# Late block tables, low parts and the shared tile of a routed decoder layer, placed anew

## The chip, the cores and the metric

The kernel runs on one core of one Trainium2 chip. The time is device microseconds of that core for the whole program, from the inputs in HBM to the output in HBM. Below, PE is TensorE, DVE is VectorE, ACT is ScalarE, POOL is GpSimd and SP is SyncE; all times inside the profiled execution are us from the start of its span.

## What is computed

One post-norm decoder layer on 1024 tokens of width 256, in fp32:

```
x = layernorm(x + attention(x))
x = layernorm(x + expert_of_token_id(x))      # 4 experts made from ctx_2048
g = silu(x @ Wg[e]);  u = x @ Wu[e];  y = (g * u) @ Wd[e]
# e: the expert with the highest router probability, 1 of 4, d_ff = 1024
x = layernorm(x + y * probability[e])
```

The change touches only the last block, the routed feed-forward with its four experts.

## The kernel before

**Tiles and items.** The tokens have been sorted by expert into a table in HBM (`x2_sorted`), in blocks of 128 rows of one expert. The last block works on T2 = 10 tiles, 0 to 9. Tiles 0 to 8 hold a block each; the last one, tile 9 (`JOINT`), is shared by two half blocks of 64 rows, which may be of two experts. The hidden width of 1024 is cut into NQ = 4 quarters. The work list `items` has 40 entries: for each quarter, tiles 0 to 9. An item is: up projection (`fup`), silu on ACT (`fsilu`), product with the second half on DVE (`fhidden`), turn of the hidden tile on PE (`fth`), its split into a high and a low part (`fhhi` on ACT, `fhlo` on DVE), down projection (`fdown`), and the sum of the quarters on DVE (`fsum`; in the last quarter `finish`, which also takes the moments of the last layernorm).

**Split precision.** Matrix products of tiles 0 to 8 are three products each: high x high, high x low, low x high (the lines 563 to 565 in `split_mm`). The weights come as 16 chunks (4 experts x 4 quarters, 768 KB each) into three staging buffers (`stage`). A chunk is split in 3 pieces of 512 columns: ACT writes the high part to `w_hi` (line 930), POOL subtracts and writes the low part to `w_lo` (line 474). A quarter has 12 pieces. The list `share` says how many of the next quarter's pieces go behind each item of this quarter. Chunks 0 to 6 are in SBUF before the block begins; chunk 7 holds the last three pieces (the 10th to 12th) of the second quarter. The first item of a quarter waits until all low parts of that quarter are there.

**The shared tile** is multiplied in plain fp32 with weights of its own (`w32`, two transfers of 768 KB per quarter from `load_w32`), as 8 up and 8 down products on 64 columns of the array (`fup_joint`, lines 825; `fdown_joint`, line 836).

**Order written out by hand.** Every engine runs a loop over i. In step i, PE does `ftx(i+1)` (turns the next tile's rows; first quarter only), `fup(i)`, `fth(i-1)`, `fdown(i-2)`; ACT does `fxhi(i+1)`, `fsilu(i)`, `fhhi(i-1)`, then the pieces of `share`; DVE does `fxlo(i+1)`, `fhidden(i)`, `fhlo(i-1)`, then `fsum(i-2)` or `finish(i-2)`. Step 3 (`EARLY`) has an order of its own, since the rows of tile 3 come late. In steps 34 to 43 ACT also writes the normed rows (`norm_row`, line 1059) of the item four steps back, and POOL sends each finished tile to HBM with an indirect DMA (line 552), with a power of -1/2 for a later tile between them (`root`, line 478).

**Tables.** Which block a tile takes is computed on DVE. Tiles 3 to 5 (`late_tables`, then `late_offsets`) just before step 0; tiles 6 to 10 in `last_rows` at the end of step 1 (its five instructions: two for `block_table`, two for `wrapped`, one for `row_table_of`, lines 1306 to 1317); the two experts of the shared tile in `joint_tables` in step 3. The semaphore `row_table` tells SP how many of these are there: 2 is tiles 3 to 5, 3 is tiles 6 to 10, 4 is the shared tile's experts.

**SP's queue.** SP issues, strictly in this order: rows of tiles 3 to 5 behind `row_table` 2; rows of tiles 6 and 7 behind `row_table` 3; behind `row_table` 4 the two `w32` transfers, the rows of tile 8, the two halves of the rows of tile 9; then chunk 7 and the later chunks (line 329). Each row transfer (132 KB) needs its row number loaded from SBUF into a register first.

## Time and profile before

| | |
|---|---|
| median of 3 runs | 188.86 us (188.37 to 189.16) |
| the profiled execution: its own time | 189.77 us |
| its span, first to last instruction | 186.9 us |
| PE busy | 169.5 us, 91% of the span |
| PE weight loads busy | 127.6 us, 68% |
| DVE / ACT / POOL busy | 126.5 / 98.0 / 101.3 us |
| the last block, steps 0 to 41 on PE | 72.4 to 178.1 us |
| granted TensorE clock, mean | 0.982 (full until 180, half behind it) |

The profiled execution is 0.91 us longer than the median. About 2.8 us of its time lie outside the span. Busy shares are averages over stages with different limits; what a change in one stage is worth is read from the waits of that stage. PE's busy share counts a matmul's latency, and neighbouring matmuls overlap in it, so steps are measured from start to start.

### The profile page before, as it was taken

What the parts mean: (1) busy time and instruction counts of PE and PEld (TensorE: products, weight loads), DVE (VectorE), ACT (ScalarE), POOL (GpSimd) and SP (SyncE); (2) the same over time, 40 slices, a digit from 0 to 9 for tenths busy, and PEclk for the clock granted to TensorE, in tenths of its full rate; (3) what the DMA queues carried; (4) which work ended last, traced back from release to release, by engine and by line L of the source; (5) the groups of instructions that cost most, each with busy time, mean ns of one, the idle gap of its engine ahead of it and who ended that gap; (6) DMA issues with size and microseconds to landing.
All of it is one profiled execution on the core that took longest, in us unless ns stands there. A gap on an engine that the chain in (4) does not pass through costs nothing.

```text
span 186.9 us, 3756 instructions
## 1 busy us (share of the span) xinstructions
PE 169.5 (91%) x944; PEld 127.6 (68%) x944; DVE 126.5 (68%) x411; ACT 98.0 (52%) x252; POOL 101.3 (54%) x127
## 2 busy tenths in 40 slices
PE   7999998899989979799899999999999999999800
PEld 2678766468868736478686788857888677887500
DVE  3489776868778958868544464443699965888740
ACT  3258889345476543357553966652666422344430
POOL 8100766626636646557745097860688810266683
PEclk9999999999999999999999999999999999999975
DMA  5999998347999341236982475455670003511020
GB/s 139 366 339 414 381 381 340 114 129 216 388 321 407 124 122 34 76 91 226 328 298 96 150 315 172 168 168 172 256 249 5 0 0 106 234 55 57 22 81 12
DMA packets 14580, 35.28 MB, mean 189 GB/s; under 512 B 1886, under 2 KB 8416, under 8 KB 14434
## 3 DMA queue, kind: packets, MB, share of 16 engines
q1 hardware_dynamic: 12880, 31.84, 49.1%
q0 software_dynamic: 1392, 3.22, 4.7%
q8 instruction: 9, 0.15, 0.3%
q14 instruction: 9, 0.07, 0.1%
q10 hardware_dynamic: 290, 0.01, 0.1%
HBM read 26.57 MB, written 9.15 MB: 191 GB/s over the span
## 4 chain that ended last, share of the span: by engine, by line
PE 62%; DVE 15%; issue 6%; DMA 6%; POOL 5%; ACT 1%; SPq 1%; POOLq 1%; DVEq 0%; ACTq 0%
PE bank L563 12%; PE bank L565 12%; PE bank L564 11%; PE bank L740 6%; DMA rows<-x_sorted 4%; PE bank L846 4%; PE bank L717 4%; PE bank L825 3%; PE bank L571 3%; POOL rstd L478 2%; DVE stats L1202 2%; DVE buf L1199 2%; POOL out_tokens L552 2%; PE bank L836 2%; DMA x_sorted<-buf,slot 2%
## 5 line engine op out<-in xcount | busy, mean ns | idle before, releaser
L474 POOL TENSOR_TENSOR w_lo<-stage,w_hi 128x512 fp32r<-128x512 f32 x40 | 51.5, 1309 | 32.9 <-ACT w_hi L930 28.0
L1046 ACT ACTIVATE gate<-bank 128x256 f32<-128x256 f32 x40 | 15.4, 385 | 47.3 <-PE bank L565 39.8
L1453 DVE TENSOR_TENSOR hid<-bank,gate 128x256 f32<-128x256 f32 x40 | 17.0, 424 | 29.9 <-ACT gate L1046 29.7
L563 PE MATMUL bank<-w_hi,xr 128*128 x72 | 30.0, 416 | 1.3 <-issue 0.8
L564 PE MATMUL bank<-w_lo,xr 128*128 x72 | 28.4, 394 | 0.0
L565 PE MATMUL bank<-w_hi,xr 128*128 x72 | 28.4, 394 | 0.0
L930 ACT ACTIVATE w_hi<-stage 128x512 fp32r<-128x512 f32 x45 | 26.7, 631 | 1.7 <-DMA stage<-in_w_ffn 1.1
L478 POOL TENSOR_TENSOR rstd<-mv,mhalf 128x1 f32<-128x1 f32 x18 | 10.9, 608 | 28.2 <-DVE mv L1192 27.2
L563 PE MATMUL bank<-w_hi,hT 128*128 x72 | 23.3, 323 | 0.0
L565 PE MATMUL bank<-w_hi,hT 128*128 x72 | 20.3, 281 | 0.0
L564 PE MATMUL bank<-w_lo,hT 128*128 x72 | 20.2, 281 | 0.0
L563 PEld LDWEIGHTS bank<-w_hi,xr 128*128 128x128 f32 x72 | 13.5, 188 | 5.6 <-issue 3.8
L846 PEld LDWEIGHTS bank<-ident,hid 128*128 128x128 f32 x80 | 10.6, 140 | 9.5 <-issue 4.6
L846 PE MATMUL bank<-ident,hid 128*128 128x128 f32 x80 | 15.6, 277 | 1.2 <-issue 0.9
L518 POOL DMA_INDIRECT x_sorted<-buf,slot x11 | 11.1, 1006 | 8.5 <-DVE slot L1301 3.9
L565 PEld LDWEIGHTS bank<-w_hi,xr 128*128 128x128 f32 x72 | 13.5, 188 | 3.1
L1461 DVE TENSOR_TENSOR hT<-bank,hT 128x256 fp32r<-128x256 f32 x36 | 15.0, 416 | 0.3 <-ACT hT L1054 0.3
L564 PEld LDWEIGHTS bank<-w_lo,xr 128*128 128x128 f32 x72 | 13.6, 189 | 1.6
L571 PE MATMUL bank<-ones 128*128 128x512 bf16 x47 | 13.2, 432 | 1.1 <-POOL ones L426 1.1
L563 PEld LDWEIGHTS bank<-w_hi,hT 128*128 128x128 f32 x72 | 13.6, 189 | 0.2 <-issue 0.2
L564 PEld LDWEIGHTS bank<-w_lo,hT 128*128 128x128 f32 x72 | 13.7, 190 | 0.0
L552 POOL DMA_INDIRECT out_tokens<-buf,outidx x10 | 10.3, 1031 | 6.2 <-issue 3.8
(214 smaller groups left out, 349.7 us busy)
## 6 DMA issues: line engine op xcount, KB each, us to landing
stage<-in_w_ffn SPq DMA_DIRECT2D x15, 768.0 KB
arena<-in_w_ffn SPq DMA_DIRECT2D x8, 768.0 KB, 4.9
rows<-x_sorted SPq DMA_DIRECT2D x20, 132.0 KB, 2.7
x_sorted<-xr SPq DMA_DIRECT2D x2, 1056.0 KB, 6.8
x_sorted<-xr SPq DMA_DIRECT2D x1, 1584.0 KB
buf<-in_x_tok SPq DMA_DIRECT2D x1, 1024.0 KB, 10.5
w_hi<-in_ctx SPq DMA_DIRECT2D x1, 1024.0 KB, 11.5
w_hi<-in_ctxT SPq DMA_DIRECT2D x1, 1024.0 KB
```

Source lines behind the costliest of these rows:

```text
L474: g.tensor_tensor(out=lo, in0=src, in1=hi.bitcast(F32), op=ALU.subtract).then_inc(split_lo, 1)
L478: g.tensor_tensor(out=rstd[:, buf, i:i + 1], in0=mv[:, buf, i, 1:2], in1=mhalf[:, 0:1], op=ALU.pow).then_inc(rstd_ready, 1)
L552: g.indirect_dma_start(out=out, out_offset=bass.IndirectOffsetOnAxis(ap=outidx[:, t:t + 1], axis=0), in_=buf[:, t, 0:D], in_offset=None, b ...
L563: mm(dst, xhi, whi, start=start, stop=False)
L564: mm(dst, xhi, wlo, start=False, stop=False)
L565: return mm(dst, xlo, whi, start=False, stop=stop)
L571: mm(bank[2][:, :].rearrange("p (a b) -> p a b", a=4), ones[:], idle_rhs, start=True, stop=True)
L846: last = tr(fH[j % 2][:, k * P:(k + 1) * P], hid[:, (T + j) % 2, k * P:(k + 1) * P], ident[:])
L930: a(hi, src, ACT.Copy).then_inc(split_hi, 1)
L1046: a(gate[:, (T + j) % 2, :], fA[j % 2][:, 0:FQ], ACT.Silu).then_inc(silu_done, 1)
L1453: v.tensor_tensor(out=hid[:, (T + j) % 2, :], in0=fA[j % 2][:, FQ:2 * FQ], in1=gate[:, (T + j) % 2, :], op=ALU.mult).then_inc(h_done, 1)
L1461: v.tensor_tensor(out=hT[:, j % 2, 1, :], in0=fH[j % 2][:, 0:FQ], in1=hT[:, j % 2, 0, :].bitcast(F32), op=ALU.subtract).then_inc(hlo_done, 1)
```

## The change

Three things, and what goes with them:

1. **Tables.** `late_offsets` (tiles 3 to 5) moves from before step 0 into step 1, behind `fxlo(2)`. `last_rows` is cut in two: `last_blocks` (two instructions) stays in step 1, the other three stay under the name `last_rows` and move to step 3, behind `fxlo(4)` and ahead of `joint_tables`. On SP the rows of tile 8 move from behind the `w32` transfers to behind those of tile 7.
2. **Pieces.** `share` becomes a list for each quarter. In the first quarter pieces begin in step 2 and go as 1, 1, 2, 2, 2, 2, 2; in the second and third they begin with the quarter's first item and end with one piece in its ninth. ACT's wait before it overwrites a half of `w_hi` asks for one item less (`y_done` ... - 1), since the shared tile doesn't read `w_hi`.
3. **Last quarter.** The order of tiles becomes 0 to 5, 9, 6, 7, 8 (`last_order`). `finish`, `norm_row` and the stores count by place n and take the tile from `last_order`.

Nothing is added to the arithmetic: each engine has as many instructions as before.

```diff
--- before.py
+++ after.py
@@ -305,16 +305,21 @@
         Q_PIECES = E * PIECES
 
 
-        share = [0, 1, 2, 1, 2, 1, 2, 1, 2, 0]
-        assert sum(share) == Q_PIECES and len(share) == T2
-
-        def quarter_pieces(q, t):
-            a = q * Q_PIECES + sum(share[:t])
-            return range(a, a + share[t])
+        share = [[0, 0, 1, 1, 2, 2, 2, 2, 2, 0], [1, 1, 2, 1, 2, 1, 2, 1, 1, 0], [1, 1, 2, 1, 2, 1, 2, 1, 1, 0]]
+        assert all(sum(n) == Q_PIECES and len(n) == T2 for n in share)
+
+        def pieces_beside(j):
+            q, n = divmod(j, T2)
+            if q == NQ - 1:
+                return range(0)
+            a = (q + 1) * Q_PIECES + sum(share[q][:n])
+            return range(a, a + share[q][n])
 
         CONSTS = 25
 
-        items = [(q, t) for q in range(NQ) for t in range(T2)]
+        in_order = list(range(T2))
+        last_order = in_order[:JOINT - 3] + [JOINT] + in_order[JOINT - 3:JOINT]
+        items = [(q, t) for q in range(NQ) for t in (last_order if q == NQ - 1 else in_order)]
         block = ctx.enter_context(nc.Block())
 
 
@@ -391,7 +396,7 @@
                     r[t] = first_row(t)
                 routed_row(t, r[t])
             sp.wait_ge(row_table, 3)
-            for t in range(LATE, JOINT - 1):
+            for t in range(LATE, JOINT):
                 routed_row(t, first_row(t))
 
             def load_w32(q):
@@ -404,7 +409,6 @@
             sp.wait_ge(row_table, 4)
             joint = [sp.value_load(joint_expert[0:1, h:h + 1], min_val=0, max_val=(E - 1) * P) for h in range(2)]
             load_w32(0)
-            routed_row(JOINT - 1, first_row(JOINT - 1))
             for h in range(2):
                 r = sp.value_load(row2[0:1, JOINT + h:JOINT + h + 1], min_val=0, max_val=(BLOCKS2 - 1) * P)
                 sp.dma_start(rows[h * SMALL:(h + 1) * SMALL, JOINT, :], scr2[bass.ds(r, SMALL), :]).then_inc(d_rows[JOINT], 16)
@@ -539,16 +543,14 @@
             for t in range(ROUTED, T):
                 scatter2(t)
 
-            for q in range(NQ):
-                for t in range(T2):
-                    if q < NQ - 1:
-                        for k in quarter_pieces(q + 1, t):
-                            split(k)
+            for j in range(len(items)):
+                for k in pieces_beside(j):
+                    split(k)
             root(LN3, 0, 0)
-            for t in range(T2):
-                if t + 1 < T2:
-                    root(LN3 + t + 1, (t + 1) % 2, 0)
-                pool.wait_ge(out_ready, t + 1)
+            for n, t in enumerate(last_order):
+                if n + 1 < T2:
+                    root(LN3 + n + 1, (n + 1) % 2, 0)
+                pool.wait_ge(out_ready, n + 1)
                 g.indirect_dma_start(out=out, out_offset=bass.IndirectOffsetOnAxis(ap=outidx[:, t:t + 1], axis=0),
                                      in_=buf[:, t, 0:D], in_offset=None, bounds_check=TOKENS - 1,
                                      oob_is_err=False).then_inc(d_out, 16)
@@ -926,7 +928,7 @@
                 else:
                     act.wait_ge(d_chunk[slot(n)], 16 * filling(n))
                 if n >= E:
-                    act.wait_ge(y_done, T + (n // E - 1) * T2)
+                    act.wait_ge(y_done, T + (n // E - 1) * T2 - 1)
                 a(hi, src, ACT.Copy).then_inc(split_hi, 1)
 
             act.wait_ge(consts, CONSTS)
@@ -1053,11 +1055,12 @@
                 else:
                     a(hT[:, j % 2, 0, :], fH[j % 2][:, 0:FQ], ACT.Copy).then_inc(hhi_done, 1)
 
-            def norm_row(t):
-
-                act.wait_ge(nmr_ready, t + 1)
-                a(buf[:, t, 0:D], buf[:, t, 0:D], ACT.Identity, bias=nmr[:, t % 2:t % 2 + 1],
-                  scale=rstd[:, t % 2, 0:1]).then_inc(out_ready, 1)
+            def norm_row(n):
+
+                t = last_order[n]
+                act.wait_ge(nmr_ready, n + 1)
+                a(buf[:, t, 0:D], buf[:, t, 0:D], ACT.Identity, bias=nmr[:, n % 2:n % 2 + 1],
+                  scale=rstd[:, n % 2, 0:1]).then_inc(out_ready, 1)
 
             fxhi(0)
             for i in range(len(items) + 4):
@@ -1075,14 +1078,11 @@
                         fxhi(i + 1)
                     if 1 <= i <= len(items):
                         fhhi(i - 1)
-                t = i - 4 - (len(items) - T2)
-                if t >= 0:
-                    norm_row(t)
+                if i - 4 >= len(items) - T2:
+                    norm_row(i - 4 - (len(items) - T2))
                 if i < len(items):
-                    q, t = items[i]
-                    if q + 1 < NQ:
-                        for k in quarter_pieces(q + 1, t):
-                            split(k)
+                    for k in pieces_beside(i):
+                        split(k)
                 if i == T2:
                     act.wait_ge(lshift_ready, 1)
                     a(lexp[:, 0:T2], lshift[:, 0:T2], ACT.Exp).then_inc(lexp_done, 1)
@@ -1358,8 +1358,10 @@
                 expert_table(EARLY, LATE)
                 offset_table(EARLY, LATE)
 
+            def last_blocks():
+                block_table(LATE, T, LATE - EARLY, nth_by_size[:], 2 * BLOCKS)
+
             def last_rows():
-                block_table(LATE, T, LATE - EARLY, nth_by_size[:], 2 * BLOCKS)
                 wrapped(LATE, T)
                 row_table_of(LATE, T)
 
@@ -1444,7 +1446,6 @@
             fxlo(1)
             early_chosen()
             late_tables()
-            late_offsets()
 
 
             def fhidden(j):
@@ -1489,16 +1490,17 @@
                 step(v.reciprocal(topw[:, 0:T2], lsum[:, 0:T2]))
                 step(v.tensor_copy(outidx[:, 0:T2], rows[:, 0:T2, TOK]))
 
-            def finish(t):
-
-                dve.wait_ge(y_done, T + len(items) - T2 + t + 1)
+            def finish(n):
+
+                t = last_order[n]
+                dve.wait_ge(y_done, T + len(items) - T2 + n + 1)
                 r = buf[:, t, 0:D]
-                v.scalar_tensor_tensor(out=r, in0=fY[(len(items) - T2 + t) % 2][:, 0:D], scalar=topw[:, t:t + 1],
+                v.scalar_tensor_tensor(out=r, in0=fY[(len(items) - T2 + n) % 2][:, 0:D], scalar=topw[:, t:t + 1],
                                        in1=acc[:, t, :], op0=ALU.mult, op1=ALU.add).then_inc(y_read, 1)
-                dve.wait_ge(y_read, T + len(items) - T2 + t + 1)
-                step(v.bn_stats(stats[:, t % 2, :], r))
-                step(v.bn_aggr(mv[:, t % 2, 0, :], stats[:, t % 2, :]))
-                variance_eps(t % 2, 0).then_inc(var_ready, 1)
+                dve.wait_ge(y_read, T + len(items) - T2 + n + 1)
+                step(v.bn_stats(stats[:, n % 2, :], r))
+                step(v.bn_aggr(mv[:, n % 2, 0, :], stats[:, n % 2, :]))
+                variance_eps(n % 2, 0).then_inc(var_ready, 1)
 
             def finish_norm(t):
                 dve.wait_ge(rstd_ready, LN3 + t + 1)
@@ -1512,11 +1514,14 @@
                     fhlo(i - 1)
                     fxlo(i)
                     fxlo(i + 1)
+                    last_rows()
                     joint_tables()
                     fhidden(i)
                 else:
                     if 1 <= i and i + 1 < JOINT and i + 1 != EARLY:
                         fxlo(i + 1)
+                    if i == 1:
+                        late_offsets()
                     if i < len(items):
                         fhidden(i)
                     if i + 1 == JOINT:
@@ -1524,7 +1529,7 @@
                     if 1 <= i <= len(items):
                         fhlo(i - 1)
                 if i == 1:
-                    last_rows()
+                    last_blocks()
                 if i == EARLY + 1:
                     last_offsets()
                 if 2 <= i <= len(items) + 1 - T2:
```

**The order on each engine.** Line numbers of the changed program differ by a few.

DVE, steps 1 to 3, from the row table of tiles 6 to 10 on (`hid` is `fhidden`, `hT` is `fhlo`, `xr` is `fxlo`; of the table, `arena` to `row`, the last three are `last_rows` of the change).

Before:

```order
L1306 TENSOR_TENSOR arena<-nth_by_size,tile_no 128x320
L1308 TENSOR_REDUCE block_no<-arena 128x5
L1312 TENSOR_SCALAR block_wrap<-block_no 128x5
L1314 TENSOR_TENSOR block_no<-block_no,block_wrap 128x5
L1317 SCALAR_TENSOR_TENSOR row<-block_no,ones_f 128x5
L1453 TENSOR_TENSOR hid<-bank,gate 128x256
L1461 TENSOR_TENSOR hT<-bank,hT 128x256
L1468 COPY arena<-bank 128x256
L1461 TENSOR_TENSOR hT<-bank,hT 128x256
L1381 TENSOR_TENSOR xr<-bank,xr 128x256 x2
```

The change:

```order
L1306 TENSOR_TENSOR arena<-nth_by_size,tile_no 128x320
L1308 TENSOR_REDUCE block_no<-arena 128x5
L1454 TENSOR_TENSOR hid<-bank,gate 128x256
L1462 TENSOR_TENSOR hT<-bank,hT 128x256
L1469 COPY arena<-bank 128x256
L1462 TENSOR_TENSOR hT<-bank,hT 128x256
L1383 TENSOR_TENSOR xr<-bank,xr 128x256 x2
L1312 TENSOR_SCALAR block_wrap<-block_no 128x5
L1314 TENSOR_TENSOR block_no<-block_no,block_wrap 128x5
L1317 SCALAR_TENSOR_TENSOR row<-block_no,ones_f 128x5
L1323 TENSOR_TENSOR past<-block_no,expert_from 128x6
L1325 TENSOR_REDUCE expert<-past 128x2
```

The three instructions `block_wrap`, `block_no` and `row` no longer stand ahead of the `hid` of step 2, but behind the `xr` of tiles 3 and 4; the experts of the shared tile (`past`, `expert` and one more) follow them directly.

SP, behind the rows of tile 7 (`row` is a row number, `joint_expert` the number that selects `w32`, `arena` is `w32`).

Before:

```order
L405 TENSOR_LOAD joint_expert
L405 ISA x2
L405 TENSOR_LOAD joint_expert
L405 ISA x2
L402 ISA
L402 DMA arena<-in_w_ffn 128x1536
L402 ISA
L402 DMA arena<-in_w_ffn 128x1536
L376 TENSOR_LOAD row
L376 ISA x2
L379 ISA
L379 DMA rows<-x_sorted 128x264
```

The change:

```order
L381 TENSOR_LOAD row
L381 ISA x2
L384 ISA
L384 DMA rows<-x_sorted 128x264
L410 TENSOR_LOAD joint_expert
L410 ISA x2
L410 TENSOR_LOAD joint_expert
L410 ISA x2
L407 ISA
L407 DMA arena<-in_w_ffn 128x1536
L407 ISA
L407 DMA arena<-in_w_ffn 128x1536
```

The rows of tile 8 went from behind the two `w32` transfers to ahead of them. Chunk 7 stands behind the two halves of tile 9 in both.

ACT, from `fxhi(7)` in step 6 to the turn copy of step 8 (`w_hi` are the pieces).

Before:

```order
L1041 ACTIVATE xr<-bank 128x256
L1046 ACTIVATE gate<-bank 128x256
L1054 ACTIVATE hT<-bank 128x256
L930 ACTIVATE w_hi<-stage 128x512 x2
L1041 ACTIVATE xr<-bank 128x256
L1046 ACTIVATE gate<-bank 128x256
L1054 ACTIVATE hT<-bank 128x256
L930 ACTIVATE w_hi<-stage 128x512
L1046 ACTIVATE gate<-bank 128x256
L1039 ACTIVATE arena<-bank 128x128
L1054 ACTIVATE hT<-bank 128x256
```

The change:

```order
L1043 ACTIVATE xr<-bank 128x256
L1048 ACTIVATE gate<-bank 128x256
L1056 ACTIVATE hT<-bank 128x256
L932 ACTIVATE w_hi<-stage 128x512 x2
L1043 ACTIVATE xr<-bank 128x256
L1048 ACTIVATE gate<-bank 128x256
L1056 ACTIVATE hT<-bank 128x256
L932 ACTIVATE w_hi<-stage 128x512 x2
L1048 ACTIVATE gate<-bank 128x256
L1041 ACTIVATE arena<-bank 128x128
L1056 ACTIVATE hT<-bank 128x256
```

Step 7 now has two pieces instead of one. The second of them is the 10th of the quarter, as the only one was: the first of chunk 7. Behind it stand the `gate` and the `arena` copy (`fxhi` of the shared tile) of step 8.

## Rows read from the trace of the kernel before

**Rows 1.** Busy time by stretch: us, PE, PEld, DVE, ACT, POOL, clock, DMA share, GB/s.

```profile
88.00:90.00 2.00, 2.00 (x15) 1.82 (x14) 1.97 (x6) 1.51 (x4) 1.97 (x2) 1.00 0.99 399
...
100.00:124.00 24.00, 24.00 (x144) 19.23 (x142) 12.48 (x37) 15.47 (x35) 14.39 (x12) 1.00 0.57 192
```

**Rows 2.** Timeline of PE: start, us, instruction, [idle before <- releaser].

```profile
76.62 0.44 PE L846 MATMUL bank<-ident,hid 128*128 128x128 f32 x2 [0.93 <-issue]
...
80.30 0.44 PE L846 MATMUL bank<-ident,hid 128*128 128x128 f32 x2 [0.26 <-DVE hid L1453]
...
91.89 0.44 PE L789 MATMUL bank<-ident,rows 128*128 128x128 f32 x2 [0.44 <-DMA rows<-x_sorted]
92.73 0.49 PE L563 MATMUL bank<-w_hi,xr 128*128 x1 [0.41 <-issue]
...
97.88 1.94 PE L825 MATMUL bank<-arena 128*64 128x512 f32 x8
```

**Rows 3.** Timeline of DVE, steps 0 to 3.

```profile
76.14 0.42 DVE L1453 TENSOR_TENSOR hid<-bank,gate 128x256 f32<-128x256 f32 x1
...
79.82 0.42 DVE L1453 TENSOR_TENSOR hid<-bank,gate 128x256 f32<-128x256 f32 x1
...
82.36 0.42 DVE L1381 TENSOR_TENSOR xr<-bank,xr 128x256 fp32r<-128x256 f32 x1 [0.42 <-ACT xr L1041]
```

**Rows 4.** Timeline of SP's queue: rows of tiles 6 and 7, then `w32`.

```profile
81.06 0.34 SPq L379 DMA_DIRECT2D rows<-x_sorted  x1
...
82.19 0.33 SPq L379 DMA_DIRECT2D rows<-x_sorted  x1
84.64 0.85 SPq L402 DMA_DIRECT2D arena<-in_w_ffn  x2
```

**Rows 5.** DMA issues at 106 and at 82: size, us to landing (median of them).

```profile
arena<-in_w_ffn SPq DMA_DIRECT2D x2, 768.0 KB, 5.0
...
rows<-x_sorted SPq DMA_DIRECT2D x1, 132.0 KB, 2.1
```

**Rows 6.** Timeline of ACT, steps 7 and 8.

```profile
96.15 0.63 ACT L930 ACTIVATE w_hi<-stage 128x512 fp32r<-128x512 f32 x1 [1.08 <-DMA stage<-in_w_ffn]
96.73 0.39 ACT L1046 ACTIVATE gate<-bank 128x256 f32<-128x256 f32 x1
```

**Rows 7.** Timelines of ACT and of PE, steps 10 to 12.

```profile
103.07 1.28 ACT L1088 ACT_TABLE_LOAD   x1
...
105.91 0.39 ACT L1046 ACTIVATE gate<-bank 128x256 f32<-128x256 f32 x1
...
107.44 0.38 PE L846 MATMUL bank<-ident,hid 128*128 128x128 f32 x2
```

**Rows 8.** Timeline of PE, first up product of the third and fourth quarters.

```profile
125.59 0.49 PE L563 MATMUL bank<-w_hi,xr 128*128 x1
...
150.56 0.49 PE L563 MATMUL bank<-w_hi,xr 128*128 x1 [0.25 <-POOL w_lo L474]
```

**Rows 9.** Timelines of ACT and POOL at the end.

```profile
174.81 0.59 ACT L1059 ACTIVATE buf<-buf,nmr,rstd 128x256 f32<-128x256 f32 x1
...
176.21 1.04 POOL L552 DMA_INDIRECT out_tokens<-buf,outidx  x1 [1.24 <-ACT buf L1059]
...
183.26 0.97 POOL L552 DMA_INDIRECT out_tokens<-buf,outidx  x1 [0.40 <-issue]
```

**Rows 10.** Busy time by stretch at the end, as rows 1.

```profile
180.00:182.00 2.00, 0.00 (x0) 0.00 (x0) 0.16 (x1) 0.73 (x2) 1.78 (x3) 0.56 0.22 77
```

**Rows 11.** Chain that ended last: start, us, what (xcount).

```profile
1.06 4.45 PE bank L571 x10
...
165.28 0.23 PE bank L563
...
172.26 1.87 PE bank L825 x8
174.13 0.38 PE bank L846 x2
```

## The prediction, made before the changed kernel ran

> **What bounds the kernel now.** I first read the busy time by stretch: from step 9 on PE has no free time (24.00 of 24.00 us between 100 and 124) at the full granted clock [rows 1]. The chain of waits says the same: steps follow each other at one pitch, (172.26 - 165.28) / 3 = 2.33 us for an ordinary item [rows 11]. PE has the same work after the change, so only time in which it stands still, or the end behind its last product, can be won. The timeline of PE has little of it in this block: 0.93 us ahead of the first turn of a hidden tile (76.62), 0.26 at 80.30, 0.44 + 0.41 for the rows of tile 8 (91.89 and 92.73) [rows 2], and the start of the fourth quarter, 0.25 [rows 8]. The last reading is of ACT: at 96.15 the first piece of chunk 7 had waited 1.08 us for its DMA, and the silu of step 8 is queued behind it, at 96.73 [rows 6]. PE's next product, of the shared tile, begins at 97.88 [rows 2]. So in step 9 two chains end together: PE's own work, and the landing of chunk 7.
>
> **The change, part by part** (minus is earlier).
>
> *Offsets of tiles 3 to 5 out of the way.* Three short DVE instructions no longer stand ahead of the first `hid` (76.14 [rows 3]); one with its step is 0.2 us, so PE's turn at 76.62 [rows 2] comes 0.6 earlier. They now run in step 1, with the `hid` there still 0.4 earlier than before.
>
> *Table of tiles 6 to 10 cut in two.* The `hid` of step 2 (79.82) no longer stands behind three table instructions; it then waits for its silu alone, and PE's 0.26 at 80.30 goes: -0.86 in all [rows 2, 3]. The rows of tile 3, which PE turns next, land some 0.4 us ahead of that, so no more is to be had here.
>
> *Rows of tile 8 ahead of `w32`.* They took their turn behind 1.5 MB. Alone such a transfer lands in 2.1 us [rows 5], well ahead of step 7: the 0.44 + 0.41 go. **PE comes to step 9 by 0.86 + 0.85 = 1.7 us earlier**, if nothing else is late: at 97.88 - 1.7 = 96.2.
>
> *What is late next.* The row table of tiles 6 to 10 is now written behind the `xr` of tile 4. That `xr` (82.36 [rows 3]) comes at 81.5; the three instructions behind it end at 82.4. Before, the rows of tile 6 were issued at 81.06 and SP had started on them some 1.1 us before, at 79.9 [rows 4]. So SP's queue starts 2.5 us later. It then has three row transfers at 1.1 us each (82.19 - 81.06), and 1.3 us for the two expert numbers and the first `w32`: 82.4 + 3.3 + 1.3 = 87.0, against 84.64 before [rows 4]. The rows of tile 6 land at 83.1 + 2.1 = 85.2, just as PE wants them (86.1 - 0.9), those of 7 and 8 with over a microsecond to spare. But chunk 7 is queued on the same 16 DMA engines behind `w32` and the rows of tile 9, and those engines are 99% busy there [rows 1]. `w32` itself has cover: issued at 87.0 and, as a pair in a quiet stretch, 5.0 us to land [rows 5], so at 92 to 93.5, wanted at 96.2.
>
> Landing of chunk 7, bounded: at the latest everything shifts by 87.0 - 84.64 = 2.4 less the 0.5 us that the rows of tile 8 took in that queue, 96.15 + 1.9 = 98.0. At the earliest `w32` lands as in the quiet stretch (its second half 5.7 us behind its issue at 87.5, so 93.2), the rows take 0.5 and 0.79 MB at 399 GB/s [rows 1] 2.0: 95.7. Before, the same sum from `w32`'s landing was passed by more than a microsecond, so I take 97.4, nearer the late end: **+1.3**. From there the chain is that of before: piece, silu, copy of the shared tile's input, up product, 97.88 - 96.15 = 1.73 [rows 2, 6]. PE would start step 9 at 99.1: 2.9 us idle, 1.3 later than before. The 1.7 won is lost, and 1.3 more. The new `share` doesn't help: the first piece of chunk 7 stays in step 7. POOL keeps up: ten pieces of 1.31 us in the five steps from 4 on, and the last three end 4.5 us behind the landing, PE wants them 4.7 behind.
>
> A page bears on this landing. The Trainium skill's page "DMA: Bandwidth & Descriptors" (Anatomy of one DMA) fits a transfer, issued from GpSimd there, by 2.0 us plus its bytes at 436 GB/s. By it `w32`, the rows of tile 9 and chunk 7 (2.5 MB) would be there 7.7 us behind 87.0, at 94.7, and the sum would be a gain (rival 1).
>
> *A piece in the quarter's first item.* In step 10 ACT now has a piece ahead of the table load for the exponential. It waits for the down products of tile 8, which end at about 103.4, and takes 0.63: the load at 103.07 becomes 104.05, the `gate` at 105.91 becomes 106.9. With `hid` behind it, PE's turn at 107.44 [rows 7] waits until 107.8: **+0.4**. Bounds 0 (were a microsecond of slack left on ACT) and 0.7.
>
> *Low parts earlier.* The third quarter starts with PE at once behind POOL: its first product takes 0.49 instead of 0.23, and 0.06 waits: -0.3. The fourth also has 0.25 + 0.15 of waiting: -0.6 [rows 8, 11]. With one piece less at the end POOL (1.3 us a piece) is done over 1 us ahead. **-0.9**; bounds -0.4 (the waits alone) and -1.0.
>
> *The shared tile as seventh.* Its `w32` lands at about 162, now wanted at 165.3: covered; without that cover it would cost what it is late. The end is POOL's: from 176.21 on it sends five tiles and takes three powers without a pause, to 183.26 [rows 9]. That run starts when the norm of the sixth tile (174.81) is done, which stands on ACT behind the silu of the last item. Ahead of that silu PE now has the shared item's up and down products and an ordinary up product, where it had the shared up product alone. The shared up with the turn behind it is 1.87 + 0.38 = 2.25 [rows 11], an ordinary one 6 x 0.23 + 0.22 = 1.62; the shared down is about 1.2, an ordinary one 0.7. So the silu of the last item comes 0.63 + 0.5 later for what is new ahead of it and 0.47 earlier for the shorter up product that it waits for. So POOL's run starts **+0.6** later and ends as much later; PE's own end (178) is not what counts. Bounds 0 and 0.7: a gain is excluded, since POOL's eight instructions stay.
>
> **Sum:** 1.3 + 0.4 - 0.9 + 0.6 = +1.4 us, on the profiled execution's 189.77: 191.2. The median of the runs is 0.9 lower, 188.86: **190.3 us**. About 0.5% (0.94 us) is what a measurement of this kernel can tell from no change.
>
> **Rivals.**
> 1. *Chunk 7 comes in time: faster.* If its queue runs without a pause from 1.4 us behind the first `w32` issue, 2.5 MB at 399 GB/s [rows 1] end at 94.6, and ACT's piece delays PE by 0.2 at most, not 2.9. Then -1.5 + 0.4 - 0.9 + 0.6 = -1.4: 187.5. It decides from a landing before about 95.1 on. Against it: by the same sum before, chunk 7 would have landed at 92.6, and it was 96.15 [rows 6]. This is also what the skill's fit gives; by that rule, too, the landing before would have been over 3 us earlier than the trace has it.
> 2. *It lands about when it did: no change.* At 95.7 to 96.3 the gain on PE is just eaten: -0.4 to +0.2, with +0.1 of the rest: 188.5 to 189.2.
> 3. *The clock falls in the gap.* PE ended its last product at 178.1, and in 180 to 182 the granted clock is 0.56, half speed, 1.2 of 2.4 GHz [rows 10]. 2.9 us idle in step 9 are longer than that. At the start of the program the ten filling products of 512 columns took 4.45 us [rows 11], 0.445 each, which is 1.2 GHz. At half speed for that long, or for half as long, PE loses 2.2 or 1.1 us: 191.4 to 192.5. For it: the length of the gap. Against it: PE is busy right before and behind it.
> 4. *The tables don't get out of the way* (the change isn't felt in step 0): PE gains 0.2, the rest stays: about 190.3 too, since chunk 7 decides.
>
> **How the numbers follow.** Forecast (with rival 4) 0.55, its own range 189.4 to 191.2; rival 1 0.14; rival 2 0.20; rival 3 0.11. Slower by over 0.5%: nearly all of the forecast and rival 3, 0.62. Same: rival 2 and the forecast's low edge, 0.24. Faster: 0.14. The range leaves out half of rival 1 and the last of rival 3: 187.6 to 192.3.
>
> **What would show it.** In the timeline of PE: no idle time at the rows of tile 8, but nearly 3 us ahead of the first product of the shared tile (line 825 before), which starts at about 99. On ACT: a piece that waits some 3.5 us for `stage`. On SP: first `w32` issue at 87. No wait for POOL at the fourth quarter. At the end: the first of five unbroken stores about 2 us later than 176.21. I am wrong if that ACT wait is under 2 us, or if the stores at the end start no later against PE's last items.

## The result, and the profile after

The changed kernel took **189.5 us** (median of 20 runs, 188.48 to 191.11), the kernel before 188.34 beside it (20 runs, 186.95 to 190.29): ratio **1.0066, 95% interval 1.0041 to 1.009**, so 0.8 to 1.7 us slower. The forecast was 190.3 on a median of 188.86, 1.4 more. The profiled execution took 190.2 us, with a span of 188.5 (before 189.77 and 186.9). The spans differ by 1.5 us, the executions' own times by 0.4, since what lies around the span was 2.8 us before and 1.7 now. The medians decide. Below, medians are over all executions and ratios over those within 1.5% of their kernel's fastest, so the two need not agree exactly (of f6's twelve, five lie above).

The block's first `gate` (the silu of step 0) stands at 74.58 in this trace and at 74.11 in that of before. Only 0.05 of these 0.47 us come from work ahead of the block, as the last product that this gate waits for shows. First the change, then before:

```profile
73.74 0.39 PE L567 MATMUL bank<-w_hi,xr 128*128 x1
```

```profile
74.58 0.39 ACT L1048 ACTIVATE gate<-bank 128x256 f32<-128x256 f32 x1 [2.06 <-PE bank L567]
```

```profile
73.68 0.39 PE L565 MATMUL bank<-w_hi,xr 128*128 x1
```

```profile
74.11 0.39 ACT L1046 ACTIVATE gate<-bank 128x256 f32<-128x256 f32 x1 [1.65 <-PE bank L565]
```

The other 0.42 is a signal of PE that comes late in this trace (the last section has more of it). Places are given as counted from the first gate, and from the product ahead of it where that matters.

Busy time by stretch, the answer to [rows 1] and [rows 10], and the stretch with the new gap (us, PE, PEld, DVE, ACT, POOL, clock, DMA share, GB/s):

```profile
96.00:99.00 3.00, 1.49 (x12) 1.09 (x12) 1.14 (x4) 2.08 (x6) 1.55 (x3) 1.00 1.01 377
...
100.00:124.00 24.00, 23.53 (x139) 18.81 (x136) 11.52 (x35) 15.02 (x35) 15.29 (x13) 1.00 0.56 184
...
180.00:182.00 2.00, 0.00 (x0) 0.00 (x0) 1.31 (x5) 0.99 (x2) 1.78 (x3) 0.98 0.09 28
```

PE was busy for all of 100 to 124 before; now 0.47 us are missing there. From 96 to 99 it works half the time, the DMA engines are full, and the granted clock stays 1.00, the 2.4 GHz level, in the gap and behind it. In 180 to 182, right behind PE's last product, it is 0.98 here, where it was 0.56 before with PE done 1.7 us earlier (178.06 for 179.74).

Timeline of PE, the places of [rows 2] (the first turn of a hidden tile, the `hid` of step 2, the rows of tile 6, the shared up product):

```profile
76.08 0.44 PE L848 MATMUL bank<-ident,hid 128*128 128x128 f32 x2 [0.34 <-issue]
...
79.59 0.44 PE L848 MATMUL bank<-ident,hid 128*128 128x128 f32 x2
...
86.02 0.44 PE L791 MATMUL bank<-ident,rows 128*128 128x128 f32 x2 [0.31 <-DMA rows<-x_sorted]
86.87 0.49 PE L565 MATMUL bank<-w_hi,xr 128*128 x1 [0.41 <-issue]
...
98.58 0.65 PE L827 MATMUL bank<-arena 128*64 128x512 f32 x2 [1.51 <-issue]
```

The waits at the `hid` of step 2 and at the rows of tile 8 are gone. In their place stand a pair of the same shape at the rows of **tile 6**, 0.31 + 0.41, and 1.51 us ahead of the shared up product. It begins at 98.58, 0.70 later than before: 0.23 later counted from the first gate, 0.65 counted from the product ahead of that gate. The second wait of the pair, marked `issue`, follows from the first: PE's own queue reads the next item's weight offset into a register (line 796, started at 86.02 beside the turn) only once the wait for the rows is over, and the up product can start 0.85 us behind that.

Timelines of DVE, answering [rows 3], and of SP's queue, answering [rows 4]:

```profile
75.60 0.42 DVE L1454 TENSOR_TENSOR hid<-bank,gate 128x256 f32<-128x256 f32 x1
...
81.65 0.42 DVE L1383 TENSOR_TENSOR xr<-bank,xr 128x256 fp32r<-128x256 f32 x1 [0.41 <-ACT xr L1043]
...
82.39 0.17 DVE L1317 SCALAR_TENSOR_TENSOR row<-block_no,ones_f 128x5 int32<-128x5 f32 x1
```

```profile
83.71 2.55 SPq L384 DMA_DIRECT2D rows<-x_sorted  x3
87.60 0.85 SPq L407 DMA_DIRECT2D arena<-in_w_ffn  x2
89.21 1.82 SPq L414 DMA_DIRECT2D rows<-x_sorted  x2
91.07 0.58 SPq L334 DMA_DIRECT2D stage<-in_w_ffn  x1
```

The row table is ready at 82.56 and SP's queue follows it: rows of tile 6 at 83.71 instead of 81.06, first `w32` at 87.60 instead of 84.64, chunk 7 at 91.07.

Timeline of ACT, steps 7 and 8, answering [rows 6]: the piece of chunk 7 waits for its transfer, and the silu and the copy of the shared tile's input stand right behind it.

```profile
96.92 0.63 ACT L932 ACTIVATE w_hi<-stage 128x512 fp32r<-128x512 f32 x1 [2.12 <-DMA stage<-in_w_ffn]
97.46 0.36 ACT L1048 ACTIVATE gate<-bank 128x256 f32<-128x256 f32 x1
97.72 0.27 ACT L1041 ACTIVATE arena<-bank 128x128 f32<-128x128 f32 x1
```

Timelines of ACT and of PE, steps 10 to 12, answering [rows 7]:

```profile
104.19 0.63 ACT L932 ACTIVATE w_hi<-stage 128x512 fp32r<-128x512 f32 x1 [0.44 <-PE bank L567]
104.84 1.28 ACT L1088 ACT_TABLE_LOAD   x1
...
107.68 0.38 ACT L1048 ACTIVATE gate<-bank 128x256 f32<-128x256 f32 x1
```

```profile
108.58 0.44 PE L848 MATMUL bank<-ident,hid 128*128 128x128 f32 x2 [0.28 <-DVE hid L1454]
108.99 0.38 PE L565 MATMUL bank<-w_hi,hT 128*128 x1
...
110.15 0.49 PE L565 MATMUL bank<-w_hi,xr 128*128 x1 [0.18 <-issue]
```

The table load is 1.77 later (0.70 of it from step 9), the turn 1.14, and the up product behind it, at 108.37 before, 1.78. PE loses more behind the late turn than at it. The low part of item 10's hidden tile, which the product at 108.99 needs, is also late, since on DVE it stands behind the late `hid`:

```profile
108.44 0.41 DVE L1462 TENSOR_TENSOR hT<-bank,hT 128x256 fp32r<-128x256 f32 x1
```

Timeline of PE, first up products of the third and fourth quarters, answering [rows 8]; then the last norm on ACT and the first and last of the five unbroken stores on POOL, answering [rows 9]:

```profile
127.13 0.40 PE L565 MATMUL bank<-w_hi,xr 128*128 x1
...
151.62 0.40 PE L565 MATMUL bank<-w_hi,xr 128*128 x1
```

```profile
176.32 0.60 ACT L1062 ACTIVATE buf<-buf,nmr,rstd 128x256 f32<-128x256 f32 x1
```

```profile
177.72 1.04 POOL L554 DMA_INDIRECT out_tokens<-buf,outidx  x1 [1.18 <-ACT buf L1062]
...
184.83 0.97 POOL L554 DMA_INDIRECT out_tokens<-buf,outidx  x1 [0.40 <-issue]
```

The chain of waits that ended last names the two places of the block that weren't in it before: PE's gap ahead of the shared up product, and the table loads on ACT.

```profile
97.07 1.51 issue
...
104.84 0.70 ACT L1088
...
106.38 1.28 ACT L1048
```

No wait for POOL is left at the fourth quarter. The run of five stores starts 1.51 us later and keeps its length (first to last start 7.11, before 7.05).

**Two lengths for all kernels.** A single time scatters by 1 to 2 us, too coarse for terms of half a microsecond. I therefore read from each kernel's one profiled execution the *front*, from the first gate to the shared up product of step 9, and the *back*, from there to the first of the five stores. Before: 97.88 - 74.11 = 23.77 and 176.21 - 97.88 = 78.33. Now: 24.00 and 79.14. Behind the first of those stores all fourteen traces have 10.73 to 10.77 us.

| kernel | ratio to before [95%] | front | back |
|---|---|---|---|
| before | 1 | 23.77 | 78.33 |
| the change | 1.0066 [1.0041, 1.009] | 24.00 | 79.14 |
| e1 tables alone | 1.0057 [1.0023, 1.0091] | 23.78 | 78.35 |
| e2 pieces alone | 0.9956 [0.992, 0.9992] | 22.87 | 78.60 |
| e3 last order alone | 1.0007 [0.9974, 1.0039] | 23.00 | 78.93 |
| f1 change, row table early | 1.0024 [0.9992, 1.0056] | 22.92 | 79.03 |
| f2 change, no piece in item 10 | 1.0044 [1.0004, 1.0084] | 24.32 | 78.06 |
| f4 rows of tile 8 ahead alone | 0.9947 [0.992, 0.9974] | 22.31 | 78.35 |
| f6 change, piece of chunk 7 later | 1.0068 [1.0035, 1.0101] | 22.68 | 80.63 |
| e4 fast start | 0.989 [0.9843, 0.9938] | 22.43 | 77.51 |
| g4 fast start again | 0.9921 [0.9891, 0.995] | 22.49 | 77.58 |
| g3 fast start, last order | 0.9922 [0.9892, 0.9953] | 23.26 | 78.09 |
| g1 row 8 and pieces | 0.9907 [0.9876, 0.9937] | 22.93 | 77.54 |
| g2 and offsets later | 0.9881 [0.9845, 0.9918] | 22.13 | 77.53 |

The back repeats to within 0.1 us between kernels that agree there (before, e1, f4: 78.33 to 78.35; e4, g1, g2, g4: 77.51 to 77.58). The front scatters by a few tenths or more with the transfers, though e4 and g4, which are the same kernel, agree within 0.06.

The front also depends on its first gate. In eleven traces that gate starts 0.04 us behind the end of the product it waits for, in the change 0.45, in e1 0.25, in e3 0.48, so those three fronts are 0.2 to 0.4 too short. Counted from the start of that product they are 24.8 (the change), 24.4 (e1) and 23.9 (e3); before has 24.2, e2 23.3, f2 24.7.

### The profile page after: what moved, and what is told of

It reads as the page before. It is cut to its first block, busy times and chain, and to the rows that moved or that the text cites. A ratio compares the mean times of both kernels' runs of the same rounds, so it can differ in the third digit from the quotient of the medians.

```text
span 188.5 us, 3756 instructions
## 1 busy us (share of the span) xinstructions
PE 169.3 (90%) x944; PEld 127.1 (67%) x944; DVE 126.1 (67%) x411; ACT 97.8 (52%) x252; POOL 100.8 (54%) x127
## 4 chain that ended last, share of the span: by engine, by line
PE 62%; DVE 13%; issue 8%; DMA 7%; POOL 4%; ACT 2%; SPq 1%; POOLq 1%; DVEq 0%; ACTq 0%
PE bank L565 13%; PE bank L567 12%; PE bank L566 12%; PE bank L719 5%; PE bank L848 5%; PE bank L827 4%; PE bank L742 4%; DMA rows<-x_sorted 3%; DMA x_sorted<-buf,slot 2%; DMA arena<-in_xT 2%; POOL out_tokens L554 2%; POOL rstd L482 2%; PE bank L838 2%; DVE stats L1202 1%; DVE buf L1199 1%
## 5 line engine op out<-in xcount | busy, mean ns | idle before, releaser
L565 PE MATMUL bank<-w_hi,hT 128*128 x72 | 23.3, 324 | 0.7 <-DVE hT L1462 0.7
L1056 ACT ACTIVATE hT<-bank 128x256 fp32r<-128x256 f32 x36 | 13.7, 380 | 0.5 <-PE bank L848 0.5
```

The source lines that it names most:

```text
L565: mm(dst, xhi, whi, start=start, stop=False)
L1056: a(hT[:, j % 2, 0, :], fH[j % 2][:, 0:FQ], ACT.Copy).then_inc(hhi_done, 1)
```

## The experiments

My theory at this point: chunk 7 lands late because SP's queue starts late, and ACT's order passes that on to PE. The rival: the late queue costs little, and the pieces and the last order are what is paid for. The first four kernels took the change apart, the next four moved one thing each, the last four tested the sum of what had been learnt.

### e1: the tables alone

The first on SP, the others on DVE:

```diff
-            for t in range(LATE, JOINT - 1):
+            for t in range(LATE, JOINT):
...
-            late_offsets()
...
+                    last_rows()
                     joint_tables()
...
+                    if i == 1:
+                        late_offsets()
...
-                    last_rows()
+                    last_blocks()
```

> The kernel before with the first part alone: offsets and row table of the late tiles placed as in the change, rows of tile 8 ahead of w32; pieces and last quarter as before. Theory (chunk 7's landing decides step 9): PE wins about 1 us up to step 7, the first w32 issue moves from 84.6 to about 87.5, chunk 7 lands about 0.8 us later than before, and the first product of the shared tile starts 0.7 later than before although nothing ahead of it on PE is late; the whole is +0.5 to +0.9 us, ratio 1.003 to 1.005. Rival (the loss of the change comes from its other parts, the tables are a gain as meant): -1 us, ratio 0.995.

Measured: 189.44 us, ratio 1.0057. First `w32` issue 13.39 us behind the first gate (before 10.53), landing of chunk 7 at 95.44, 22.11 behind it, PE idle for 1.15 us ahead of the shared up product; the wait for the rows of tile 6 is here too. So the part of the change that was to free PE in the first steps makes the kernel slower on its own, though against the profile of before the front is the same (23.78 to 23.77; from PE's product 0.2 longer). That looked like a contradiction until e2 and e3 came. The ratio is just above the 1.003 to 1.005 that I gave; the rival, a gain, is out.

### e2: the pieces alone

```diff
-        share = [0, 1, 2, 1, 2, 1, 2, 1, 2, 0]
+        share = [[0, 0, 1, 1, 2, 2, 2, 2, 2, 0], [1, 1, 2, 1, 2, 1, 2, 1, 1, 0], [1, 1, 2, 1, 2, 1, 2, 1, 1, 0]]
```

> The kernel before with the second part alone: new lists of pieces and the wait for one item less. Theory: step 9 as before (chunk 7's first piece stays in step 7), +0.4 to +1.0 us in steps 10 to 12 since a piece stands ahead of the two table loads on ACT, -0.3 at the third quarter's start, -0.6 at the fourth's: -0.3 to +0.3 in all, ratio 0.998 to 1.002. Rival (low parts were what mattered): -0.9, ratio 0.995. Rival (later pieces in the first quarter make POOL late for the second): over +1 us with a wait of PE for POOL at step 10.

Measured: 187.71 us, ratio 0.9956, faster by 0.2 to 1.5 us. The back is 78.60, +0.27: the low parts' gain less what item 10 costs. The ratio is below the 0.998 to 1.002 that I gave and near the rival's 0.995 (only the low parts matter). The time and this length don't point the same way, so by them the gain would lie in the front, which one profiled execution can't price. One part is seen: PE has no idle time ahead of its turn at 79.31, where it had 0.26 before. f2 and e4 settle the two terms of the back.

### e3: the last order alone

```diff
+        last_order = in_order[:JOINT - 3] + [JOINT] + in_order[JOINT - 3:JOINT]
```

> The kernel before with the third part alone: tiles of the last quarter in the order 0 to 5, 9, 6, 7, 8. Theory: everything to 165 us is as before; the last silu comes 0.6 us later, POOL's run of five stores starts 0.6 later and the end is +0.6, ratio 1.003. Rival (the shared tile early takes PE's last wait out of the end): -0.3 to -0.5. Rival (end bound by the DMA alone): 0.

Measured: 188.42 us, ratio 1.0007, inconclusive by the clock (forecast 1.003). The back is 78.93, +0.60.

**What e2 and e3 say of the kernel before.** Both have its tables and its SP queue, and their fronts are 22.87 and 23.00, not 23.77. Chunk 7 landed 19.75 and 20.04 us behind the first gate in them, and 22.02 in the profile of before, though it was issued at 14.79 and 14.70, there at 15.09. The trace of before shows why: fifteen of the sixteen parts of that chunk are there by 94.65, and one at 96.13; the chunk behind it has the same straggler, fifteen by 96.55 and one at 97.99. The trace of the change has no such gap (96.41 and 96.90 are its last two). So the landing on which the prediction was built was itself delayed by 1.5 us by one of its sixteen parts. Kernels with the tables of before have a front of about 23.2 (mean of the three), those with the change's (the change, e1, f2) one of 24.0: **+0.8 us**. Counted from PE's product it is +0.9, and +1.1 if the disturbed trace of before is left out. The times give less: take each kernel's difference to before in time, and from it that of its back; what is left is the difference of the fronts. Over the thirteen kernels this puts the front of before, from PE's product, at 24.0 on average (23.4 to 24.9), and the term at +0.6. That is an estimate, and says that before's typical execution isn't as undisturbed as e2's and e3's. The term is +0.6 to +1.1.

### f1: the change with the row table early

```diff
-                    last_rows()
                     joint_tables()
...
+                if i == 2:
+                    last_rows()
```

> The changed kernel with one edit: the row table of tiles 6 to 10 is computed in step 2, right behind the low part of hidden tile 1, and no longer behind the input of tile 4. Theory (SP's queue starts late, so chunk 7 lands late, and its first piece on ACT holds the silu in front of the shared tile): counted from the first gate of the block, the first w32 issue comes 1.4 to 2 us earlier than in the changed kernel (there 13.0 behind that gate), chunk 7 lands earlier by about as much, the idle 1.5 us of PE ahead of the shared up product shrinks to under 0.4, and the waits for the rows of tile 6 go: 1.0 to 1.6 us gained on the changed kernel, so a ratio of 0.997 to 1.001 to the kernel before. Rival (the pieces' order and the last quarter cost it all, the late queue nothing): the time stays at that of the changed kernel, ratio 1.006.

Measured: 187.9 us, ratio 1.0024, 0.8 us under the change's by the two ratios; it is above my 0.997 to 1.001, and its interval takes in both 1.0 and part of the change's. The profiled execution was the longest of the twelve (190.68), and its block began late (first gate 76.25): the mean granted clock is 0.96 from 17 to 60 us, ahead of the block, and 1.00 in it, from 60 to 180. So of this execution only lengths inside the block count. The front fell from 24.00 to 22.92. SP's queue, ACT and PE:

```profile
88.49 0.85 SPq L407 DMA_DIRECT2D arena<-in_w_ffn  x2
```

```profile
97.51 0.63 ACT L932 ACTIVATE w_hi<-stage 128x512 fp32r<-128x512 f32 x1 [0.76 <-DMA stage<-in_w_ffn]
```

```profile
99.17 0.65 PE L827 MATMUL bank<-arena 128*64 128x512 f32 x2 [0.16 <-issue]
```

`w32` is issued 12.24 us behind the first gate instead of 13.02 (I had expected 1.4 to 2 us; the change's first gate is late, and from the third gate it is 7.81 instead of 8.96). PE's idle time ahead of the shared tile is 0.16 instead of 1.51, the wait for the rows of tile 6 is gone. Three DVE instructions, moved up a step, give that back, so the late queue was what cost it. e4 and g4, with the same edit, have fronts of 22.43 and 22.49. The rival would have left the time at 1.006, and the front at 24.

### f2: the change with no piece beside item 10

```diff
-        share = [[0, 0, 1, 1, 2, 2, 2, 2, 2, 0], [1, 1, 2, 1, 2, 1, 2, 1, 1, 0], [1, 1, 2, 1, 2, 1, 2, 1, 1, 0]]
+        share = [[0, 0, 1, 1, 2, 2, 2, 2, 2, 0], [0, 2, 2, 1, 2, 1, 2, 1, 1, 0], [1, 1, 2, 1, 2, 1, 2, 1, 1, 0]]
```

> The changed kernel with one edit: in the second quarter no piece is split beside the first item (the list for it reads 0, 2, 2, 1, 2, 1, 2, 1, 1, 0). Theory: ACT comes to the table load for the exponential 0.9 to 1.1 us earlier, PE's pauses in steps 10 to 12 go and the time falls by 0.8 to 1.0 us, ratio about 1.002 to the kernel before. The prediction had 0.4 for this term; by it the ratio would be 1.004. Rival (POOL then ends its pieces of that quarter later and PE waits for it at item 20): no gain, and a wait of PE for POOL in front of item 20.

Measured: 188.37 us, ratio 1.0044. The back fell by 79.14 - 78.06 = 1.08 us, as expected; the time fell by 0.4 only, which is what I had put down for the prediction's smaller term (1.004), with an interval that reaches over both. What decides between them is that the length repeats: from the shared up product to the up product at 110.15 the change, e2 and f1, which all have that piece, take 11.56 to 11.58 us, and the ten kernels without it 10.48 to 10.53 (f6, held by POOL, left out). ACT and PE in steps 10 to 12:

```profile
103.13 1.28 ACT L1088 ACT_TABLE_LOAD   x1
```

```profile
107.50 0.38 PE L848 MATMUL bank<-ident,hid 128*128 128x128 f32 x2
107.64 0.36 PE L565 MATMUL bank<-w_hi,hT 128*128 x1
...
108.44 0.49 PE L565 MATMUL bank<-w_hi,xr 128*128 x1
```

From the shared up product (97.94) the table load is 5.19 us away, in the change 6.26, before 5.19. PE has no pause at any of the three places, and POOL isn't waited for at item 20.

### f6: the first piece of chunk 7 a step later

```diff
-        share = [[0, 0, 1, 1, 2, 2, 2, 2, 2, 0], [1, 1, 2, 1, 2, 1, 2, 1, 1, 0], [1, 1, 2, 1, 2, 1, 2, 1, 1, 0]]
+        share = [[0, 0, 1, 1, 2, 2, 2, 1, 3, 0], [1, 1, 2, 1, 2, 1, 2, 1, 1, 0], [1, 1, 2, 1, 2, 1, 2, 1, 1, 0]]
```

> The changed kernel with one edit: the first piece of chunk 7 is split beside item 8 instead of item 7 (the first quarter's list ends 2, 2, 2, 1, 3, 0), so the silu that the shared tile's input stands behind no longer waits for that transfer. Theory (the transfer holds PE through ACT's order): the 1.5 us of idle time of PE ahead of the shared up product go. But POOL's last three low parts, 1.3 us each, still end about 4.5 us behind the landing, so item 10 waits for POOL: 0.7 to 1.5 us of what is won come back there, net gain 0 to 0.8 us, ratio 1.002 to 1.006. Rival (PE waits for w32 itself or for something else than ACT's piece): the idle time ahead of the shared up product stays above 1 us.

Measured: 188.99 us, ratio 1.0068, no gain (I had given 1.002 to 1.006, 0 to 0.8 us of it). ACT, POOL and PE:

```profile
93.92 0.39 ACT L1048 ACTIVATE gate<-bank 128x256 f32<-128x256 f32 x1 [1.14 <-PE bank L567]
...
94.82 1.67 ACT L932 ACTIVATE w_hi<-stage 128x512 fp32r<-128x512 f32 x3
```

```profile
95.53 3.75 POOL L478 TENSOR_TENSOR w_lo<-stage,w_hi 128x512 fp32r<-128x512 f32 x3 [1.37 <-ACT w_hi L932]
```

```profile
99.42 0.49 PE L565 MATMUL bank<-w_hi,xr 128*128 x1 [1.33 <-POOL w_lo L478]
```

The silu of step 8 runs before the landing (chunk 7 lands at 94.80), and PE starts the shared tile without a pause: the front is 22.68, 1.32 shorter. One step on, the first product of the second quarter waits 1.33 us for POOL, which can't start its last three low parts before the chunk is there. The back is 80.63, 1.49 longer. The landing binds PE by two paths that are within 0.2 us of each other; moving the piece only changes which. The rival, that PE waited for `w32` itself, is out.

### f4: only the rows of tile 8 ahead of `w32`

```diff
-            for t in range(LATE, JOINT - 1):
+            for t in range(LATE, JOINT):
                 routed_row(t, first_row(t))
...
             load_w32(0)
-            routed_row(JOINT - 1, first_row(JOINT - 1))
```

> The kernel before with one edit: SP issues the rows of tile 8 ahead of the shared tile's weights w32 instead of behind them. Bytes and their number are the same in front of chunk 7. Theory (from the other profiles chunk 7 lands 19.8 to 20.0 us behind the first gate of the block, 2 us ahead of what the profile of the kernel before showed): PE's two waits for those rows go, 0.4 to 0.85 us, and little stands against it: ratio 0.9955 to 0.998. Rival (the landing of chunk 7 is the bound in the kernel before too): the waits go and the same time comes back ahead of the shared up product, ratio 1.000.

Measured: **186.15 us, ratio 0.9947**, faster by 0.5 to 1.5 us and by more than the 0.9955 to 0.998 that I gave. The front is 22.31. SP's queue, ACT and PE:

```profile
83.48 0.85 SPq L402 DMA_DIRECT2D arena<-in_w_ffn  x2
```

```profile
92.94 0.63 ACT L929 ACTIVATE w_hi<-stage 128x512 fp32r<-128x512 f32 x1 [0.68 <-DMA stage<-in_w_ffn]
93.93 0.39 ACT L1045 ACTIVATE gate<-bank 128x256 f32<-128x256 f32 x1 [0.35 <-PE bank L564]
```

```profile
89.80 0.38 PE L788 MATMUL bank<-ident,rows 128*128 128x128 f32 x2
```

The rows of tile 8 are there when PE comes, and `w32` stands only 10.71 us behind the first gate (before 10.53): the transfer that was put ahead of it costs it nearly nothing. Chunk 7 is issued even earlier, 14.19 to 15.09. Its piece waits 0.68 us, but the silu behind it waits for PE afterwards, so nothing is passed on. This one edit of the change is a gain; the rival (bound by chunk 7 before, too) is refuted.

### e4 and g4: a fast start

The change with f1's edit (the row table in step 2), the last order of before, and other lists:

```diff
+        share = [[0, 0, 0, 2, 2, 2, 2, 2, 2, 0], [0, 2, 2, 1, 2, 1, 2, 1, 1, 0], [1, 1, 2, 1, 2, 1, 2, 1, 1, 0]]
+        last_order = in_order
```

> The changed kernel with (a) the last three instructions of the row table in step 2 behind fhlo instead of step 3, (b) pieces of the first quarter from step 3 on, 2 each in steps 3 to 8, (c) no piece in the first item of the second quarter, 2 in each of the next two, (d) the last quarter in its old order. Theory: row table 3 at about 80.4, first w32 issue at 85.0 to 85.6, chunk 7 issued when POOL has chunk 4's third low part, about 88.7, and landing at 93.5 to 95; PE starts the shared tile at 96.2 to 96.8 instead of 97.9 before and 98.6 in the change; no stall by the table loads; quarter starts as in the change; end as before: -2 to -2.6 us against before, ratio 0.986 to 0.990. Rival (chunk 7 lands at 96 or later whenever it is issued, the DMA stream being the bound): -0.9 us, ratio 0.995.

> The version with a fast start once more, beside its twin with the change's last order and the two others of this batch: 0.987 to 0.991 of the kernel before, as measured before with six runs. It is the base against which the last order's price is read.

Measured: 186.36 us, ratio 0.989, and again 186.11 us, 0.9921 (seven runs; the second is outside the 0.987 to 0.991 that I gave, its interval isn't). In e4 the first `w32` is issued at 85.23, chunk 7 lands at 94.08 and the shared up product starts at 96.26, each inside the band given; the rival (a landing at 96 or later) is out. Backs 77.51 and 77.58: against 78.33 the low parts alone are worth 0.8.

### g3: the fast start with the change's last order

```diff
-        last_order = in_order
+        last_order = in_order[:JOINT - 3] + [JOINT] + in_order[JOINT - 3:JOINT]
```

> The version with a fast start (ratio 0.989 before) with one edit: the shared tile is the seventh item of the last quarter, as in the change. No transfer is late in this kernel. Theory (ACT's last norm stands behind 0.6 us more of PE's work): from the shared tile's up product in step 9 to the first of the five unbroken stores 0.6 us more, and the ratio 0.003 higher than that version's in the same batch. Rival (nothing at the end changes, as the single change's 1.0007 leaves open): 0.000.

Measured: 185.97 us, ratio 0.9922, against 0.9921 of its twin: by the clock no difference where I had expected 0.003, with intervals of 0.003 on each side. Back 78.09, +0.51 on g4. The first of the five stores, in g3 and then in g4:

```profile
174.09 1.04 POOL L554 DMA_INDIRECT out_tokens<-buf,outidx  x1 [1.18 <-ACT buf L1062]
```

```profile
172.88 1.04 POOL L554 DMA_INDIRECT out_tokens<-buf,outidx  x1 [1.25 <-ACT buf L1062]
```

Three pairs give this length (e3 on before 0.60, g3 on g4 0.51, and the change with f2's item 10, 78.06, on 77.5: 0.5). It is shown in the traces and not in the times, whose intervals are wider than it.

### g1 and g2: what is left if the gains are kept and the delay isn't

g1 is the kernel before with f4's edit and e4's lists of pieces. g2 is g1 and, on DVE:

```diff
-            late_offsets()
...
+                    if i == 1:
+                        late_offsets()
```

> The kernel before with two edits: the rows of tile 8 ahead of w32 on SP, and the pieces spread as in the version with a fast start (first quarter 0, 0, 0, 2, 2, 2, 2, 2, 2, 0; second 0, 2, 2, 1, 2, 1, 2, 1, 1, 0; third 1, 1, 2, 1, 2, 1, 2, 1, 1, 0). Tables and last order as before. Theory: the gains are in different places and add up, 1.0 us in the front half (0.9947 alone) and 0.8 us behind the shared tile (78.33 us from its up product to the five stores become 77.5): ratio 0.988 to 0.992, and the tables of the change are worth nothing more than this. Rival (the tables' delay is needed for the gain of the version with a fast start, 0.989): only 0.993 to 0.996.

> As the kernel with rows of tile 8 ahead and new pieces, and one edit more: the three DVE instructions for the offsets of tiles 3 to 5 stand in step 1, ahead of the hidden tile there, and no longer ahead of the first hidden tile. SP's queue starts no later by that. Theory (the prediction's first term): PE turns the first hidden tile 0.6 us earlier, nothing is late next, and the time falls by 0.3 to 0.6 us more, 0.002 to 0.003 in the ratio. Rival (PE of step 0 waits for something else, or the time comes back at the next hidden tile): within 0.1 us of the other kernel.

Measured: g1 186.17 us, ratio 0.9907, in the expected band: the tables of the change aren't needed for the gain. g2 **185.36 us, ratio 0.9881 [0.9845, 0.9918]** (six runs), 0.0026 below g1, as its theory had it, though the intervals overlap. Front 22.13, the shortest of all. PE's first turn of a hidden tile and the issue of `w32` in g2:

```profile
74.47 0.44 PE L846 MATMUL bank<-ident,hid 128*128 128x128 f32 x2 [0.27 <-DVE hid L1450]
```

```profile
82.66 0.85 SPq L405 DMA_DIRECT2D arena<-in_w_ffn  x2
```

g2 has the change's good parts: rows of tile 8 first, the offsets out of the way, and low parts earlier, but the row table where it was, and no piece in item 10. `w32` is issued 10.04 us behind the first gate, where the change has 13.02. It is 2.2 us faster than the kernel before (0.0119 of 187.46), and against the change, by the two ratios, over 3.

## Why the prediction came out

The number was right: +1.4 forecast, +1.2 measured. 189.5 lies at the low edge of the forecast's own range, 189.4 to 191.2, mainly because the kernel before has a median of 188.34 over 20 runs and had 188.86 over the three that the sum started from. The mechanism was right in its main path: the row table late, so SP's queue, so chunk 7, and ACT's order hands that on to PE. That the sum came so close is in part luck, for two of its terms were mis-sized in opposite directions, the landing too large and the piece in item 10 too small, and one wait was missed.

*Offsets of tiles 3 to 5 out of the way, -0.6: right.* From the start of the last product of step 0's up projection to PE's first turn of a hidden tile the five kernels with the old place take 2.82 to 2.94 us (before, e2, e3, f4, g1), the nine with the new place 2.20 to 2.34: 0.6 us between the means.

*Table of tiles 6 to 10 cut in two, -0.26 of its -0.86: right in this trace, needless otherwise.* PE's turn in step 2 is 0.71 earlier (79.59 for 80.30), and its 0.26 of idle time [rows 2] is down to 0.06. But e2, g1 and g2 keep the table whole and have no idle time above 0.01 us there either; before, e3 and f4, which have it whole and the old lists of pieces, have 0.26 to 0.28. With the new lists no low part runs on POOL in step 1, and the table's first instruction behind the reduction takes 0.17 us instead of 0.62 (below). The cut saves a stall that an emptier POOL saves as well, and the row table's delay was the price of it.

*Rows of tile 8 ahead of `w32`, -0.85: right*, and worth a ratio of 0.9947, 1.0 us, alone.

*What is late next, +1.3: the right chain, too large.* The first `w32` issue was at 87.60 (forecast 87.0: the row table was 0.16 late, and the two expert numbers took 1.67 and not 1.3). `w32` landed at 94.57, 6.45 us behind the issue of its second half at 88.12; in the quiet stretch the second half took 5.7. Chunk 7 landed at 96.90 (forecast 97.4, bounds 95.7 to 98.0), and the shared up product began at 98.58 (forecast 99.1): 0.70 later than before instead of 1.3. Against less disturbed fronts the term is +0.6 to +1.1, as e2 and e3 showed. The forecast went to the late end of its bounds because chunk 7 had landed "more than a microsecond" later than its own sum before, and 1.5 us of that was the one late part. f1, in which only the row table is early, gives the delay back, and f6 shows both ways in which the landing reaches PE.

*The rows of tile 6 "just as PE wants them": wrong, 0.72 us.* They landed at 85.98, and PE waited 0.31 + 0.41. The cost was hidden in the front, for PE then only idled less at the shared tile: it reached step 9 at 97.07 instead of the 96.2 forecast, and stood still 1.5 us instead of 2.9. So the sign that I had named, an idle time of nearly 3 us and an ACT wait of 3.5, was about half as large (1.51, 2.12), just above the 2 us under which I had called myself wrong.

*A piece in the quarter's first item, +0.4: the failed term, +1.08.* The prediction followed the late `hid` to PE's turn and stopped there. The turn is indeed 0.44 later than before, counted from the shared up product (10.00 us to 9.56). The product with `hT` then follows the turn's start by 0.42 and not by 0.14: it needs the low part of `hT`, which DVE makes behind the late `hid` (108.44 + 0.41 = 108.85), where in f2 that low part is done before PE comes. And the next up product follows by 1.16 and not by 0.80. It waits for no other engine's work: PE's queue reads its weight offset (line 796) from 109.37 on, and the product starts 0.78 us behind that. In f2 the same read stands at 107.68, 0.75 ahead of its product, but there it is hidden behind products that are running already. So a wait that empties PE's queue lays bare the register read behind it, as at the rows of tile 6. 0.44 + 0.28 + 0.36 = 1.08, the difference of f2's back. The upper bound of 0.7 was too low: it took one wait for the whole.

*Low parts earlier, -0.9: right, -0.8* (77.5 of e4, g1, g2, g4 against 78.33).

*The shared tile as seventh, +0.6: right, +0.5 to +0.6 in three pairs of traces*, not resolved by the times. The three terms of the back give 1.08 - 0.8 + 0.55 = +0.8, and the back grew by 79.14 - 78.33 = 0.81.

*The rivals.* Rival 1 (chunk 7 in time) is out: the chunk landed 9.3 us behind the first `w32` issue, in the profiles of the other changed kernels 8.7 (e1) to 10.2 (g1), in that of before 11.5. The estimate of 7.7 us for these bytes, from the fit on the Trainium skill's page "DMA: Bandwidth & Descriptors" (Anatomy of one DMA), is below every one of them. Rival 2 (a landing at 95.7 to 96.3) missed it by 0.6, the forecast by 0.5 on the other side; the full price of the table load alone would have turned its "no change" into a loss. Rival 3 (the clock falls in the gap) did not happen: 1.00 granted from 96 to 99 and from 100 to 124, with 1.51 us of idle time. A gap of 2.9 us did not come about, so the rival isn't tested for that length. Rival 4 is out: the tables are felt in step 0 (2.20 to 2.34 against 2.82 to 2.94 us above). Part of the difference between measured singles (+0.57%, -0.44%, +0.07%, sum +0.2%) and the whole (+0.66%) stays open; each has an interval of 0.3 to 0.4%.
